# A PSUM bank per tile and chunk, and a new order of all calls, in a fused attention and FP4 feed-forward kernel

## The reference, cut to what matters

```
q, k = rope(x @ Wq), rope(x @ Wk)           # 8 heads of 16
v, g = x @ Wv, x @ Wg                       # 8 heads of 32
scores = (q/4) k^T * decay_h^(i-j), causal  # no softmax
o = rmsnorm_per_head(scores @ v) * w_norm * silu(g)
x1 = layernorm(x + o @ Wo)
quant(t): per block of 16, scale = max|t|/6, round t/scale to the FP4 grid, times scale
h  = silu(quant(x1) @ quant(Wgate)^T) * (quant(x1) @ quant(Wup)^T)    # width 352
out = layernorm(x1 + quant(h) @ quant(Wdown)^T)
```

## Time and profile before

| what | value |
|---|---|
| median of 3 runs | 133.45 us (133.18 to 134.6) |
| the profiled execution | 132.9 us, its span 131.2 us |
| PE busy | 119.2 us (91%) |
| DVE busy | 110.0 us (84%) |
| ACT busy | 88.8 us (68%) |
| POOL busy | 87.7 us (67%) |
| chain that ended last, by engine | PE 66%, DVE 16%, DMA 6%, issue 4% |

### The profile page before, as it was taken

The page is one execution under the profiler, slowest core; times in us unless marked ns, Lnnn a source line. Parts: engine busy times, 40 slices in busy tenths (PEclk is TensorE's granted clock), DMA queues, the critical chain, the costliest instruction groups (busy, mean ns, idle before and its releaser), DMA issues.

```text
span 131.2 us, 5084 instructions
## 1 busy us (share of the span) xinstructions
PE 119.2 (91%) x2040; PEld 82.7 (63%) x2040; DVE 110.0 (84%) x329; ACT 88.8 (68%) x311; POOL 87.7 (67%) x124
## 2 busy tenths in 40 slices
PE   4859699989999999999999999899999999999860
PEld 4425257766667676766675576567696788887650
DVE  1249999689589999999999998899999999999810
ACT  3143847557674776839576858778696878898882
POOL 5202726577687849784783869476949797996781
PEclk9999999999999999999999999999999999999996
DMA  3899991000000000000000000000000000011222
GB/s 104 256 273 392 425 440 45 5 5 5 0 5 0 5 0 5 0 7 0 5 2 5 0 5 2 5 0 5 0 5 0 25 2 0 20 40 30 58 80 80
DMA packets 4791, 7.68 MB, mean 59 GB/s; under 512 B 800, under 2 KB 3872, under 8 KB 4512
## 3 DMA queue, kind: packets, MB, share of 16 engines
q1 hardware_dynamic: 3744, 6.60, 14.3%
q10 hardware_dynamic: 1024, 0.76, 1.8%
HBM read 6.31 MB, written 1.05 MB: 56 GB/s over the span
## 4 chain that ended last, share of the span: by engine, by line
PE 66%; DVE 16%; DMA 6%; issue 4%; ACT 3%; POOL 2%; SPq 1%; POOLq 0%; DVEq 0%
PE ps L313 7%; PE ps L441 7%; DMA tabs_sb<-rope_tables 6%; PE ps L421 6%; PE ps L427 6%; PE ps L330 5%; PE ps L307 4%; PE ps L355 4%; PE ps L365 4%; DVE probs L727 3%; PE ps L433 3%; PE ps L386 3%; PE ps L341 3%; PE ps L388 2%; PE ps L387 2%
## 5 line engine op out<-in xcount | busy, mean ns | idle before, releaser
L859 POOL TENSOR_TENSOR rstd_h<-ms,minus_half 128x8 f32<-128x8 f32 x16 | 26.8, 1672 | 6.9 <-DVE ms L743 6.8
L313 PE MATMUL ps<-w_vg,xT_sb 128*128 128x512 f32 x32 | 17.4, 625 | 1.5 <-DVE S L738 1.1
L854 POOL TENSOR_TENSOR qk<-rope 128x256 f32<-128x256 f32 x16 | 11.7, 729 | 9.7 <-DVE rope L721 9.7
L878 POOL TENSOR_TENSOR xq<-x_ratio,xs 128x128 f32<-128x128 f32 x16 | 7.8, 489 | 11.9 <-DVE x_ratio L656 11.9
L441 PE MATMUL ps<-wd_T,hT 128*128 128x128 f32 x96 | 14.1, 283 | 1.3 <-DVE r L757 0.7
L721 DVE TENSOR_TENSOR rope<-ps,tabs_sb 128x512 f32<-128x512 f32 x16 | 11.0, 687 | 4.6 <-DMA tabs_sb<-rope_tables 3.3
L870 POOL TENSOR_TENSOR rstd<-veps,minus_half 128x1 f32<-128x1 f32 x16 | 9.3, 579 | 7.7 <-DVE veps L752 7.7
L886 POOL TENSOR_TENSOR hq<-h_ratio,hs 128x352 f32<-128x352 f32 x16 | 13.0, 815 | 1.7 <-DVE h_ratio L656 1.4
L441 PEld LDWEIGHTS ps<-wd_T,hT 128*128 128x128 f32 x96 | 12.1, 191 | 3.1 <-ACT hT L483 1.5
L727 DVE TENSOR_TENSOR probs<-ps,causal 128x512 f32<-128x512 f32 x16 | 11.0, 690 | 2.8 <-PE ps L330 2.4
L421 PE MATMUL ps<-wgu_T,xqT 128*128 128x352 f32 x32 | 13.3, 496 | 0.0
(11 more groups left out here) (110 smaller groups left out, 340.1 us busy)
## 6 DMA issues: line engine op xcount, KB each, us to landing
tabs_sb<-rope_tables SPq DMA_DIRECT2D x1, 2048.0 KB, 12.0
tabs_sb<-rope_tables SPq DMA_DIRECT2D x1, 1280.0 KB, 8.1
out<-x SPq DMA_DIRECT2D x16, 64.0 KB, 1.5
tabs_sb<-rope_tables SPq DMA_DIRECT2D x1, 512.0 KB, 4.6
xT_sb<-x_transposed SPq DMA_DIRECT2D x1, 512.0 KB, 7.6
xT_sb<-x_transposed SPq DMA_DIRECT2D x1, 320.0 KB, 5.5
tabs_sb<-rope_tables SPq DMA_DIRECT2D x1, 256.0 KB, 3.6
w_vg<-in_w_vg ACTq DMA_DIRECT2D x1, 256.0 KB, 3.9
```

The lines of the kernel that those rows point to most:

```text
L313: mm(vg_ps, xT(c), w_vg[:], start=True, stop=True).then_inc(vg_pe, 1)
L854: gp.tensor_tensor(g16(qk[:, c % D, :]), g16(rope[:, c % D, 0, :]), g16(rope[:, c % D, 1, :])[:, :, ::-1, :], ALU.add).then_inc(qk_p, 1)
L859: gp.tensor_tensor(rstd_h[:, c, :], ms[:, c, :], minus_half[:], ALU.pow).then_inc(rms_p, 1)
```

## The change: what it does

`BANKS` now gives a bank for each kind of tile and each chunk (for U two banks). Scores and oT stay in banks 0 to 3. `occupy` notes which chunk filled a bank, and `free` waits for the readers of that chunk. All accesses take the chunk as an argument. The four written orders are replaced by new ones, of the same calls, with two additions: a second `warm_up(4)` on PE behind `project_qk(0)`, and in `h_ratio_` a wait for `h_value(c - 6)` on POOL, which read the ring slot. The lists are cut below to the places that the text speaks of.

```diff
-        BANKS = {"sc": (0, 1, 2, 3), "oT": (0, 1, 2, 3), "o": (1,), "yT": (7,), "qk": (4,), "qkT": (0,),
-                 "vg": (6,), "att": (5,), "xqT": (2,), "gate": (4,), "hT": (3,), "up": (7,),
-                 "down": (6,), "U": (6, 7)}
+        BANKS = {
+            "sc": (0, 0, 0, 0, 0, 0, 0, 0, 0, 0, 0, 0, 0, 0, 0, 0),
+            "oT": (0, 0, 0, 0, 0, 0, 0, 0, 0, 0, 0, 0, 0, 0, 0, 0),
+            "o": (3, 3, 3, 3, 3, 3, 0, 1, 0, 3, 3, 0, 0, 0, 0, 0),
+            "yT": (7, 4, 7, 6, 2, 3, 5, 7, 1, 5, 3, 4, 4, 4, 7, 6),
+            "qk": (1, 6, 4, 4, 7, 4, 6, 4, 4, 4, 7, 4, 4, 0, 4, 1),
+            "qkT": (0, 2, 7, 2, 0, 0, 0, 2, 2, 2, 2, 0, 2, 2, 1, 2),
+            "vg": (4, 5, 5, 6, 6, 6, 4, 6, 6, 6, 6, 7, 6, 6, 6, 6),
+            "att": (5, 5, 5, 5, 5, 5, 5, 5, 5, 5, 5, 5, 5, 6, 5, 7),
+            "xqT": (5, 6, 5, 5, 4, 1, 4, 4, 4, 4, 4, 4, 4, 4, 0, 3),
+            "gate": (4, 4, 4, 4, 4, 4, 4, 4, 4, 4, 4, 5, 3, 0, 0, 0),
+            "hT": (7, 3, 2, 7, 7, 2, 3, 2, 3, 1, 4, 7, 0, 4, 2, 4),
+            "up": (7, 7, 1, 7, 7, 6, 4, 7, 7, 3, 5, 7, 4, 4, 6, 2),
+            "down": (7, 5, 0, 1, 0, 1, 7, 2, 2, 5, 3, 5, 1, 7, 2, 7),
...
+        }
...
             def free(n):
-                name = tile.get(n)
+                name, count = tile.get(n, (None, 0))
                 if name == "sc":
-                    pe.wait_ge(mask_v, filled[name])
+                    pe.wait_ge(mask_v, count)
...
             def occupy(name, banks):
+                filled[name] += 1
                 for n in banks:
                     free(n)
-                    tile[n] = name
-                filled[name] += 1
+                    tile[n] = name, filled[name]
...
-            warm_up(4); project_qk(0); project_vg(0); transpose_qk(0); project_qk(1); state_product(0); scores(0)
-            project_vg(1); from_state(0); values(0); state_product(1); project_qk(2); transpose_qk(1); transpose_o(0)
...
-            transpose_o(1); transpose_qk(2); transpose_gate_up_weights(); state_product(2); transpose_down_weights()
-            scores(2); project_vg(4); out_projection(0); transpose_y(1); project_qk(4); from_state(2)
-            state_product(3); values(2); project_qk(5); transpose_o(2); transpose_qk(3); out_projection(1)
-            state_product(4); scores(3); project_qk(6); from_state(3); values(3); project_qk(7); transpose_qk(4)
-            transpose_o(3); transpose_y(2); transpose_xq(0); project_vg(5); gate(0); scores(4); out_projection(2)
...
-            project_vg(12); transpose_xq(7); transpose_y(9); scores(11); up(6); out_projection(9); from_state(11)
...
-            values(12); state_product(13); transpose_o(12); transpose_qk(13); transpose_y(11); project_vg(14)
...
-            down(9); up(15); gate(15); transpose_h(11); down(10); transpose_h(12); down(11); transpose_h(13); down(12)
-            transpose_h(14); down(13); down(14); transpose_h(15); down(15)
+            warm_up(4); project_qk(0); warm_up(4); project_vg(0); transpose_qk(0); state_product(0); project_qk(1)
+            scores(0); project_qk(2); project_vg(1); from_state(0); values(0); state_product(1); transpose_o(0)
...
+            values(1); transpose_y(0); transpose_o(1); transpose_gate_up_weights(); state_product(2)
+            transpose_down_weights(); scores(2); project_vg(4); project_qk(4); out_projection(0); transpose_y(1)
+            from_state(2); values(2); state_product(3); project_qk(5); transpose_o(2); transpose_qk(3); project_qk(6)
+            out_projection(1); scores(3); project_qk(7); state_product(4); from_state(3); values(3); transpose_o(3)
+            transpose_qk(4); transpose_y(2); transpose_xq(0); project_vg(5); gate(0); scores(4); out_projection(2)
...
+            transpose_y(9); project_vg(12); transpose_xq(7); scores(11); out_projection(9); up(6); from_state(11)
...
+            values(12); state_product(13); transpose_y(11); transpose_o(12); transpose_qk(13); up(8); project_vg(14)
...
+            transpose_h(10); up(15); down(9); transpose_h(11); down(10); transpose_h(12); down(11); down(12)
+            transpose_h(13); transpose_h(14); down(13); transpose_h(15); down(14); down(15)
...
-            copy_v(0); silu_g_(0); q_even(0); q_odd(0); k_transposed(0); silu_g_(1); copy_v(1); copy_oT(0); squares(0)
...
-            ln1_squares(3); copy_oT(5); magic_h(0); squares(5); silu_of_gate(1); q_odd(6); copy_yT(4); k_transposed(6)
-            q_even(6); copy_xqT(2); ln1_norm(3); copy_v(7); silu_g_(7); ln1_squares(4); copy_oT(6); magic_x(3)
...
+            copy_v(0); q_even(0); k_transposed(0); q_odd(0); silu_g_(0); copy_v(1); copy_oT(0); silu_g_(1); squares(0)
...
+            copy_oT(5); magic_x(2); silu_of_gate(1); squares(5); ln1_norm(3); q_odd(6); k_transposed(6); q_even(6)
...
             def h_ratio_(c):
+                if c >= 6:
+                    dve.wait_ge(hq_p, c - 5)
...
-            rotate(0); weights_amax(0); next_state(0, 0); next_state(0, 1); rotate(1); mask_scores(0); weights_inv(0)
-            weights_amax(1); weights_ratio(0); next_state(1, 0); rotate(2); next_state(1, 1); mean_square(0)
-            weights_inv(1); gated(0); weights_ratio(1); weights_plus(0); mask_scores(1); weights_grid(0)
...
-            h_amax(15); ln2_sum(11); h_inv(15); h_ratio(15); ln2_sum(12); h_plus(15); h_grid(15); ln2_sum(13)
-            ln2_sum(14); ln2_sum(15)
+            rotate(0); weights_amax(0); next_state(0, 0); weights_inv(0); next_state(0, 1); mask_scores(0); rotate(1)
+            weights_amax(1); rotate(2); weights_ratio(0); next_state(1, 0); weights_inv(1); mean_square(0); gated(0)
+            next_state(1, 1); weights_ratio(1); weights_plus(0); mask_scores(1); weights_grid(0); weights_value(0)
...
+            ln2_sum(8); h_inv(14); h_ratio(14); h_grid(13); h_product(15); h_plus(14); h_amax(15); ln2_sum(9)
+            h_inv(15); h_grid(14); h_ratio(15); ln2_sum(10); ln2_sum(11); h_plus(15); h_grid(15); ln2_sum(12)
```

More of the change, by code:

```diff
@@ L419, in gate @@
                 pe.wait_ge(xqT_act, c + 1)
[L420 to L421 removed]
+                occupy("gate", banks("gate", c))
+                mm(gate_ps(c), xqT[:, c % D, :], wgu_T[:, 0:I], start=True, stop=True).then_inc(gate_pe, 1)
             def up(c):
@@ L465, in _ @@
-            state_product(12); values(11); gate(7); transpose_qk(12); transpose_o(11); transpose_y(10); project_vg(13)
-            project_qk(15); up(7); transpose_xq(8); out_projection(10); scores(12); gate(8); from_state(12)
-            values(12); state_product(13); transpose_o(12); transpose_qk(13); transpose_y(11); project_vg(14)
-            transpose_xq(9); up(8); scores(13); out_projection(11); from_state(13); state_product(14); values(13)
-            gate(9); transpose_o(13); transpose_qk(14); transpose_h(0); transpose_y(12); project_vg(15); up(9)
@@ new lines, in _ @@
+            transpose_xq(2); scores(6); out_projection(4); from_state(6); state_product(7); values(6); gate(2)
+            transpose_o(6); transpose_qk(7); up(2); project_qk(10); transpose_y(5); project_vg(8); transpose_xq(3)
+            scores(7); out_projection(5); gate(3); from_state(7); state_product(8); values(7); project_qk(11)
+            transpose_o(7); transpose_qk(8); transpose_y(6); up(3); project_vg(9); scores(8); out_projection(6)
+            transpose_xq(4); from_state(8); state_product(9); values(8); gate(4); transpose_o(8); transpose_y(7)
@@ new lines, in _ @@
+            transpose_qk(9); project_vg(10); project_qk(12); transpose_xq(5); up(4); scores(9); out_projection(7)
+            from_state(9); state_product(10); values(9); gate(5); project_qk(13); transpose_y(8); transpose_o(9)
+            transpose_qk(10); up(5); project_vg(11); out_projection(8); transpose_xq(6); scores(10); gate(6)
+            from_state(10); values(10); state_product(11); project_qk(14); transpose_o(10); transpose_qk(11)
+            transpose_y(9); project_vg(12); transpose_xq(7); scores(11); out_projection(9); up(6); from_state(11)
@@ new lines, in _ @@
+            state_product(12); values(11); gate(7); transpose_y(10); transpose_qk(12); transpose_o(11); project_qk(15)
+            project_vg(13); up(7); transpose_xq(8); scores(12); out_projection(10); gate(8); from_state(12)
+            values(12); state_product(13); transpose_y(11); transpose_o(12); transpose_qk(13); up(8); project_vg(14)
+            scores(13); out_projection(11); transpose_xq(9); from_state(13); state_product(14); values(13); gate(9)
+            transpose_qk(14); transpose_o(13); up(9); transpose_h(0); transpose_y(12); project_vg(15)
@@ new lines, in _ @@
+            transpose_xq(10); scores(14); out_projection(12); gate(10); from_state(14); values(14); state_product(15)
+            transpose_y(13); transpose_o(14); transpose_qk(15); up(10); transpose_h(1); down(0); transpose_xq(11)
+            out_projection(13); scores(15); gate(11); up(11); from_state(15); values(15); transpose_y(14); down(1)
```

(2 more changed lines are left out.)

386 lines of the change are left out of this document (189 added, 197 removed).

## The result

The kernel after takes 129.1 us (median of 4 runs, 128.61 to 129.33); the kernel before, run beside it on the same chip, 134.02 (133.18 to 135.17). The ratio is 0.965, with a 95% interval of 0.959 to 0.970. The forecast was 132.0 in a range of 130.6 to 133.9: the sign was right, the size a third of what came. The profiled executions are 132.9 and 129.14 us, 3.76 apart; the rest of the distance between the medians lies in a spread of before's times that after does not show. Throughout, medians take in all executions of a kernel, and ratios leave out those more than 1.5% above its fastest.

A forecast was written before the change was run, and what follows sets the result against it. PE and DVE, busy 119.2 and 110.0 of 131.2 us, were taken to bound the kernel, both full in the middle. Terms -1.2 - 0.3 + 0 = -1.5 us against 133.45 gave 131.95, rounded 132.0; 8-in-10 range 130.6 to 133.9.

The forecast's parts named there:

- Parts 1 and 2: Start to 32 us: DVE work moves ahead of rotate(1), and PE carries a lead of -1.2 us into the full stretch.
- the signs: Trace marks named beforehand to show each claim, among them rotate(5) at 25.1 and project_vg(5) at 30.2.
- The wait for the copy behind `values(3)`: Tile 3: nothing stands between values(3) and transpose_o(3), so PE idles 0.59 us.
- The warm-up: Start, PE: the second warm_up(4) costs nothing, bounds 0 to +0.4 us; project_vg(0) no later than 6, at 1.1 us.
- Part 3: Tiles 11 and 12: own banks remove waits only where PE stood for them; -0.3 us, bounds 0 and -1.2.
- Part 4: The end: an earlier start of the last tile's chain only reorders full work; 0 us, bounds -0.4 and +0.5.
- (a): Rival: the lead carries and banks give more, down to down over ln2_sum above all; -2.8 us, 130.6; chance 0.15.
- (c): Rival, tiles 6 to 8 and 11: ACT's queue waits for POOL, 1.25 us a hit; three give 135.7; chance 0.11.
- (d): Rival: new gaps let PE's clock fall to 1.2 GHz in one 10 us stretch; near 142; chance 0.02.
- the forecast's own case: Whole kernel: the summed parts hold, range 131.2 to 132.9 by the bounds of parts 1 to 4; chance 0.50.

The follow-up runs named there:

- e16: Control: orders and banks of the kernel before, in the code of the kernel after; ratio to before 1.001.
- e12: Kernel after with four DVE calls moved one to two places, out of the way of POOL's products; 129.06 us, ratio to before 0.963.
- e11: Kernel after with POOL's gated_output and h_value each replaced by a one-column pow and a one-element product; 128.63 us, ratio to before 0.960.
- e4: Orders and banks of the kernel after up to tile 9, those of before behind it; 131.7 us, ratio to before 0.990.
- e17: Orders and banks of before in the code of after, with down(1) moved on PE from ahead of scores(15) to behind transpose_y(14); ratio to before 1.004.
- e5: Orders and banks of the kernel before up to tile 15, those of after behind it, no second warm-up; 132.02 us, ratio to before 0.987.
- e10: Kernel before with POOL's gated_output and h_value each replaced by a one-column pow and a one-element product; ratio to before 0.992.
- e9: Orders of the kernel before with a bank table fitted to them, 45 entries moved; 132.15 us, ratio to before 0.989.
- e8: Kernel after with POOL's list of the kernel before; 138.83 us, ratio to before 1.039.
- e1: Orders of the kernel before with 99 of the 112 changed bank entries as in after; 143.15 us, ratio to before 1.066.
- e2: Orders of the kernel after with 101 of the 112 changed bank entries as in before; 159.4 us, ratio to before 1.189.
- e6: Orders and banks of the kernel after up to tile 15, those of before behind it; 132.85 us, ratio to before 0.993.

## Why the prediction was right or wrong

**Right:** what the start does (`mask_scores(0)` and `weights_inv(0)` ahead of `rotate(1)`, `project_vg(0)` by 6 us at 1.1); that no transfer and no code cost is added (e16); that the full middle is PE's, with DVE's missing 1.20 us of the window 80 to 90 as its echo; the distance from `gate(15)` to `down(15)`, forecast as 8.0: `down(15)` starts 0.67 behind `down(14)`, which runs from 121.76, so it is 122.43 - 114.28 = 8.15.

**Parts 1 and 2, -1.2:** the lead at tile 9 was 0.63 in the profiled execution, since its tables landed later, and two of the signs failed in it: `rotate(5)` came at 26.04 and `project_vg(5)` at 31.12, not 25.1 and 30.2. The wait for the copy behind `values(3)` was there, 0.55 of the forecast 0.59. With earlier tables `project_vg(5)` comes at 30.36 (e12) to 30.57 (e11); in e4, e11 and e12, with the new start too, `mask_scores(1)` is 1.0 to 1.15 earlier than before. The mechanism was right, and the 0.63 just within the bound of 0.6.

**The warm-up, costed at nothing with up to +0.4.** This term was mis-sized in sign. I read one execution and took its clock as given. In part of the executions PE does its first two tiles at 1.2 GHz and is 1.3 to 2.2 us later at `mask_scores(1)`; no trace of a kernel with the second warm-up shows that. It is worth 0.8 us of before's median (133.71 to 132.88), 0.4% by the ratio, and hardly anything in a good execution.

**Part 3, -0.3, bounds 0 and -1.2:** measured -1.14 between `mask_scores(9)` and (15). The step "a bank of its own takes a wait away only where PE stood for it" looked for waits alone. 0.67 of the 1.08 us is not a wait: `out_projection(10)` and then `down(1)` stand behind their tile instead of ahead of it. I had compared the lists for the order of dependent calls, not for how much PE work stands between two masks. What is left for waits is about 0.4, near what I took; but e17, where one such call alone gave 0.1, shows that this split is a count and not a measurement.

**Part 4, 0, bounds -0.4 and +0.5:** the step that failed. Measured -2.09. That an earlier start of the chain "only reorders full work", since DVE is busy 32.8 of 34.3 us, took DVE's busy time as work. e5 shows the end shorter by 2.1 us through its own lists and banks alone (24.56 in e16, 22.46 in e5). Two things were in it. 1.43 us of DVE's busy time was DVE held by POOL's products, in four instructions that the trace of before shows at 0.49 to 0.88 us beside 0.28; the stretch is worth 0.9 of the 2.09 (e10, e11). Of the other 1.2 us, 0.2 is one `ln2_sum`, now behind `h_grid(15)`, which I had put on the debit side. The likeliest source of the rest is a wait that part 3's own rule asks for and that I looked for in tiles 11 and 12 only: PE's 1.0 us in `down` for `ln2_sum`, gone in after and in e5. Which move of the lists or banks does it is not shown: none of the end was tried alone, and in e9, which has none of these waits either, the stretch changed as well.

**The rivals.** (a) named the right places, `down` to `down` over `ln2_sum` above all, and was too small by the end. (c) and (d) did not come: ACT waited 0.4 us for POOL, and the granted clock stayed at 1.00. But e8 shows both alive, (d) behind (c), and e1 shows (d) without a change of POOL's or ACT's list. Against (a) I held that DVE had only 1.5 us to give at the end; that was the same error as in part 4. The range of the forecast's own case, 131.2 to 132.9, is also narrower than the bounds of the parts add up to: -2.95 and -0.1 against 133.45, so 130.5 to 133.35. The measured time lies outside this too.

## What to carry to other kernels

Busy time is not work: compare each instruction with the shortest of its own form, and what lies beside the long ones is a term of the sum, paid where that engine is on the chain that ended last and hardly elsewhere. Look for waits for a bank in every stretch, the end included. When orders change, count for each engine how much work stands between two marks of the critical loop, besides looking at who waits for whom. A table of banks and the lists of four engines are one design: e1, e2 and e8 each undo one part and end 7, 19 and 4% above the kernel before, so neither can be tried, or judged, alone.

## What the runs showed of the hardware

- A DVE instruction with two SBUF inputs that starts inside a POOL product of 128 columns or more, with 0.2 us of it left, ends 0.15 us (128 columns) or 0.38 us (352 columns) behind it, 126 times of 127; POOL's 1.65 us `pow` on 8 columns does not hold it.
- PE's first tiles ran at one of two speeds for a time that differs from execution to execution: `project_vg(1)` took 1.02 to 1.13 or 2.08 us. A window ahead of the first record of the granted clock reads 1.00 although its matmuls take twice as long. With eight more matmuls in a gap of 0.4 to 1.1 us ahead of `project_vg(0)`, `project_vg(1)` took 1.02 to 1.13 in all eight kernels traced.
- One idle time of PE of 2.05 us in the middle of full work was followed by a granted clock of 0.73 over 5 us, and idle times of 1.33 and 1.50 us, which ended at 16.8 and 22.3, by one of 0.50 from 23.4 to 30.2 (e1). One of 1.56 us (e6) was not followed by a fall.
